# Masked cross attention: look-ahead, order of transfers and places of small work in a sequence

## The reference, cut to what matters

```python
def _L0_xattn_ref(target, source, target_mask, source_mask, Wq, bq, Wk, bk, Wv, bv):
    # b = 8, t = s = 512, SIZE = 256, HEADS = 16, HEAD_DIM = 16
    q = jnp.einsum('oc,bct->bot', Wq, target) + bq[None, :, None]
    k = jnp.einsum('oc,bcs->bos', Wk, source) + bk[None, :, None]
    v = jnp.einsum('oc,bcs->bos', Wv, source) + bv[None, :, None]
    ...
    dot = jnp.einsum('bhdt,bhds->bhts', q, k) / math.sqrt(HEAD_DIM)
    mask = target_mask[:, :, :, None] * source_mask[:, :, None, :]
    dot = mask * dot - (1.0 - mask) * NEG
    amap = jax.nn.softmax(dot, axis=-1) * mask
    out = jnp.einsum('bhts,bhds->bhdt', amap, v)
    return out.reshape(b, HEADS * HEAD_DIM, t)
...
x = _layernorm(x + _L0_xattn_ref(x, ctx_2048, mask, mask, Wq, bq, Wk, bk, Wv, bv), axis=-1)
```

## Time and profile before

| | |
|---|---|
| median of 3 runs | 3819.51 us (3816.24 to 3822.37) |
| the profiled execution | 3825.85 us, of which span 3824.0 us |
| masked cross attention in the span | about 454 us to 1323 us |
| busy in the whole span | PE 83%, PEld 54%, DVE 44%, ACT 33%, POOL 14% |
| mean granted clock of PE | 0.896 of full speed |

### The profile page before, as it was taken

The page is one execution under the profiler, slowest core; times in us unless marked ns, Lnnn a source line. Parts: engine busy times, 40 slices in busy tenths (PEclk is TensorE's granted clock), DMA queues, the critical chain, the costliest instruction groups (busy, mean ns, idle before and its releaser), DMA issues. The chain is left out here.

```text
span 3824.0 us, 48404 instructions
## 1 busy us (share of the span) xinstructions
PE 3156.5 (83%) x16306; PEld 2066.2 (54%) x16339; DVE 1683.5 (44%) x3232; ACT 1259.3 (33%) x3220; POOL 545.7 (14%) x551
## 2 busy tenths in 40 slices
PE   6999758777777659999987888599999997899894
PEld 5666422222222147777764555488888886444441
DVE  5666535444445321211115666366666665211113
ACT  2333214343435401111103444355565553211110
POOL 1000200111011120000000000233333332300002
PEclk9999867667767679999998999799999998999997
DMA  1000174444545140000001000211122102600323
GB/s 67 14 20 22 55 129 86 90 91 98 98 84 103 54 122 12 23 12 12 12 22 36 22 22 17 74 59 45 50 78 67 45 33 99 239 0 33 121 86 109
DMA packets 124210, 235.40 MB, mean 62 GB/s; under 512 B 10808, under 2 KB 23608, under 8 KB 124048
## 3 DMA queue, kind: packets, MB, share of 16 engines
q1 hardware_dynamic: 104928, 190.19, 18.6%
q0 software_dynamic: 7664, 27.40, 2.1%
q10 hardware_dynamic: 11456, 15.66, 1.3%
HBM read 161.55 MB, written 71.14 MB: 61 GB/s over the span
## 5 line engine op out<-in xcount | busy, mean ns | idle before, releaser
L1256 DVE TENSOR_REDUCE x_minus_max<-banks 128x2 f32<-128x1024 f32 x256 | 310.4, 1222 | 417.9 <-PE banks L1320 412.2
L1192 ACT ACTIVATE x_probs<-banks 128x512 f32<-128x512 f32 x512 | 287.7, 595 | 383.4 <-PE banks L1338 314.7
L1338 PE MATMUL banks<-x_stacked_q,x_stacked_k 53*128 53x512 f32 x512 | 267.9, 591 | 94.8 <-ACT x_probs L1192 68.5
L1338 PEld LDWEIGHTS banks<-x_stacked_q,x_stacked_k 53*128 53x128 f32 x512 | 106.0, 232 | 361.5 <-issue 190.5
L481 ACT ACTIVATE a_probs<-banks,a_minus_max 128x128 f32<-128x128 f32 (+1 forms) x512 | 209.0, 426 | 145.0 <-DVE a_minus_max L564 143.3
L1320 PE MATMUL banks<-x_stacked_k,x_stacked_q 51*128 51x512 f32 x512 | 217.7, 552 | 34.0 <-DMA x_stacked_q<-x_mask_parts_dram 28.6
L1350 PE MATMUL banks<-x_probs,x_v 128*32 128x512 f32 x1024 | 188.7, 819 | 5.4 <-ACT x_probs L1192 5.4
L2137 ACT ACTIVATE x_probs<-banks,x_minus_max,x_rroot 128x256 f32<-128x256 f32 x256 | 143.1, 567 | 91.4 <-DVE x_minus_max L2248 91.4
L2073 POOL TENSOR_TENSOR x_probs<-x_probs,x_inverse 128x512 f32<-128x512 f32 x128 | 133.1, 1040 | 275.6 <-DVE x_inverse L2282 275.6
L564 DVE TENSOR_REDUCE a_minus_max<-banks 128x2 f32<-128x512 f32 (+1 forms) x192 | 131.9, 687 | 82.3 <-remote 54.8
L2807 DVE TENSOR_TENSOR m_h<-banks,m_silu 128x512 f32<-128x512 f32 x39 | 27.0, 692 | 318.8 <-PE banks L2923 165.6
(11 more groups left out here) (369 smaller groups left out, 7737.6 us busy)
## 6 DMA issues: line engine op xcount, KB each, us to landing
x_parts_dram<-x_parts SPq DMA_DIRECT2D x16, 1024.0 KB, 5.4
x_x<-x_after SPq DMA_DIRECT2D x24, 512.0 KB, 4.4
x_stacked_k<-x_parts_dram SPq DMA_DIRECT2D x48, 256.0 KB
x_stacked_q<-x_parts_dram SPq DMA_DIRECT2D x48, 256.0 KB
x_after<-a_z SPq DMA_DIRECT2D x16, 512.0 KB, 2.7
x_z<-x_after SPq DMA_DIRECT2D x16, 512.0 KB, 6.6
x_heads_dram<-x_heads_out SPq DMA_DIRECT2D x32, 256.0 KB, 2.2
x_after<-x_z SPq DMA_DIRECT2D x16, 512.0 KB, 2.8
```

The source lines that it names most:

```text
L1192: act.activation(probs[:, n % 8, :], psum[at.bank(f"exp{n}")], ACT.Exp, scale=SCALE)\
L1256: dve.tensor_reduce(minus_max[:, c % 2, h % 4:h % 4 + 2, t], at.pair(use), AX.X, ALU.max, negate=True)\
L1338: ins = pe.matmul(psum[at.bank(use)], stacked[1][u][rows, h // 2, s * P:(s + 1) * P].bitcast(F32R), stacked[0][u][rows, h // 2, :].bitcast ...
```

## The change

Only this block is touched. Four things are changed. Scores run 36 slots ahead, so that score' begins at slot 28. Maxima and shifts move with them: the shift rows of a head group are now sent 17 slots before their first exp (slots 15, 31, 47, 63), and were sent 9 slots before (slots 7, 23, 39, 55). `stack` is split in two portions of four head pairs, with semaphores of their own; `load_inputs` stands between the portions and `load_rows` behind them. And the pieces of projection move from slots 24, 28, 40 and 44 to 34, 38, 42 and 51, the values pieces from 9 and 14 to 6 and 19.

```diff
-UNIT_LEAD = 28
+UNIT_LEAD = 36
 UNITS_IN_TAIL = 1
-MAXIMA_AT = 4
-SHIFT_AT = 7
+MAXIMA_AT = 12
+SHIFT_AT = 15
 SLOTS = 4 * 16
-PIECES_AT = (24, 28, 40, 44)
-VALUES_AT = (9, 14)
+PIECES_AT = (34, 38, 42, 51)
+VALUES_AT = (6, 19)
...
-            if q in (at, at + 16, at + 32):
-                add((kind, (q - at) // 16 + 1))
-            if q == at + 48:
-                add((kind + "'", 0))
+            if q in (at, at + 16):
+                add((kind, (q - at) // 16 + 2))
+            if q in (at + 32, at + 48):
+                add((kind + "'", (q - at) // 16 - 2))
...
-            def stack(b, u):
-                sp.wait_ge(parts_written, b * 32 + 32)
+            def stack(b, u, part):
                 for w in (1, 0):
                     for half in range(2):
                         for j, pair in enumerate(STACKED_PAIRS):
-                            sp.dma_start(stacked[w][u][HALF * half + CH * j:HALF * half + CH * (j + 1)],
-                                         parts_dram[w, u, pair[w]].rearrange("(h g d) s -> g d h s", g=2, d=CH)[half])\
-                                .then_inc(stacked_ready[w][u], 16)
+                            sp.dma_start(stacked[w][u][HALF * half + CH * j:HALF * half + CH * (j + 1), 4 * part:4 * part + 4],
+                                         parts_dram[w, u, pair[w], part * P:(part + 1) * P].rearrange("(h g d) s -> g d h s", g=2, d=CH)[half])\
+                                .then_inc(stacked_ready[w][u][part], 16)
...
                 if following:
-                    stack(b + 1, 1 - u)
+                    sp.wait_ge(parts_written, b * 32 + 64)
+                    stack(b + 1, 1 - u, 0)
+                if own and second:
+                    sp.wait_ge(v_ready, b * 2 + 2)
+                    load_inputs(b + 2, u)
+                if following:
+                    stack(b + 1, 1 - u, 1)
                 if own:
                     if not (isinstance(b, int) and b < 2):
                         sp.wait_ge(stored[u], at.in_turn * 16)
                     load_rows(b, u)
-                if own and second:
-                    sp.wait_ge(v_ready, b * 2 + 2)
-                    load_inputs(b + 2, u)
...
-                        if n == 0:
+                        if n in (0, 16):
                             for w in range(2):
-                                pe.wait_ge(stacked_ready[w][to], at.loads(ahead) * 8 * 16)
+                                pe.wait_ge(stacked_ready[w][to][n // 16], at.loads(ahead) * 8 * 16)
```

More of the change, by code:

```diff
@@ L961, in cross_attention_masked @@
         parts_written = sem("parts_written")
-        stacked_ready = [[sem(f"stacked_ready_{w}{u}") for u in range(2)] for w in "qk"]
+        stacked_ready = [[[sem(f"stacked_ready_{w}{u}{part}") for part in range(2)] for u in range(2)] for w in "qk"]
         v_ready = sem("v_ready")
@@ L1061, in stack @@
                         for j, pair in enumerate(STACKED_PAIRS):
-                            sp.dma_start(stacked[w][u][HALF * half + CH * j:HALF * half + CH * (j + 1)],
-                                         parts_dram[w, u, pair[w]].rearrange("(h g d) s -> g d h s", g=2, d=CH)[half])\
-                                .then_inc(stacked_ready[w][u], 16)
-                        sp.dma_start(stacked[w][u][HALF * half + STACKED_MASK:HALF * half + STACKED_MAX],
-                                     mask_dram[w, b].unsqueeze(1).broadcast_to([len(STACKED_PAIRS), H // 2, POS]))\
-                            .then_inc(stacked_ready[w][u], 16)
+                            sp.dma_start(stacked[w][u][HALF * half + CH * j:HALF * half + CH * (j + 1), 4 * part:4 * part + 4],
+                                         parts_dram[w, u, pair[w], part * P:(part + 1) * P].rearrange("(h g d) s -> g d h s", g=2, d=CH)[half])\
+                                .then_inc(stacked_ready[w][u][part], 16)
+                        sp.dma_start(stacked[w][u][HALF * half + STACKED_MASK:HALF * half + STACKED_MAX, 4 * part:4 * part + 4],
+                                     mask_dram[w, b].unsqueeze(1).broadcast_to([len(STACKED_PAIRS), H // 4, POS]))\
+                            .then_inc(stacked_ready[w][u][part], 16)
             def write_heads(b, u, c):
@@ L1261, in run @@
                         by_tile = minus_max[:, n % 2].rearrange("p (i g) t -> p t g i", g=2)
-                        at.wait_free(dve, f"score{8 * n + 7}" if kind == "maxima" else "score'7")
+                        at.wait_free(dve, f"score{8 * n + 7}" if kind == "maxima" else f"score'{8 * n + 7}")
                         high_part(dve, max_parts[:, :, :, 0, :], by_tile).then_inc(max_steps, 1)
```

## The result

The changed kernel takes 3694.7 us (median of 4 runs, 3690.0 to 3699.3), and the kernel before 3817.9 in the same comparison. The ratio is 0.968, with a 95% interval of 0.966 to 0.970. That is 123 us less, where I had forecast 98 (3721 us, range 3685 to 3765). The profiled execution took 3689.95 us with a span of 3688.1, 135.9 less than the span of the earlier trace rows. It is the quickest of the four runs, so its terms add up to more than the medians show.

What follows compares the result with a forecast made beforehand. No engine is full, so the order of waits bounds it, chiefly PE's for context and shift rows. Savings 87.5 + 6.2 + 4.5 = 98.2 us take the profiled 3825.85 to 3727.7, 6.3 over the median: 3721 us, range 3685 to 3765.

Steps and rivals of the forecast that it cites:

- Both waits: PE's waits for the context (69.1 us, nearly all in batches 1 to 5) and the shift rows (25.1 us) go.
- ACT's wait: At slot 24, for the inverse sums written at slot 20: PE's 5.8 us charged to each of batches 1 to 5, 29 us.
- A gain that hangs on the slot more than on the order: Projection pieces: from slot 34 even inputs landing no earlier (+45.9 us) would leave a wait of only 4 us.
- I put all this at nothing: Splitting `stack` in portions: 16 more transfers at 0.44 us issue each, 7 us, later second portion and z; cost nothing.
- the opening: Lead sequence before batch 0: first portion lands after 16.3 us, first exp at 542.3 instead of 546.8, 4.5 us gained.
- Rival C: Finer transfers are slow: portions land at +48 us, 116 us lost against 98 gained, 3837 us; chance 0.03.
- Pieces at nothing: New places of the projection pieces: work moved, not changed; still two pairs of neighbours four slots apart, so no effect.
- the middle batch: Batches 1 to 5: 89.7 us each, from batch 0's 87.0 less 3.1 plus 5.8, against 107.2; 87.5 us saved.
- 6.4 from the clock: Batches 1 to 5: the saving per batch beyond the waits, from a clock of 0.79 instead of 0.69.
- The rest: Outside batches 1 to 5: batches 0 and 6 lose shift waits, 6.2 us; first exp 4.5 us earlier; batch 7 unchanged.

Runs made afterwards that it cites:

- e4: The changed kernel with ACT's read of the inverse rows, and the wait ahead of it, at slot 29 instead of 24: 3674.2 us.
- e1: The changed kernel with the old order of transfers (both portions of stacked rows, z, then the inputs), its slots kept: 3698.1 us.
- e2: The kernel before with only the new order of transfers, in two portions; look-ahead 28, old shift and piece slots: 3705.2 us.
- e10: The kernel before with its stacked rows cut into two portions of half-size transfers, old order and slots kept: 3763.6 us.
- e5: The changed kernel with the projection pieces back at slots 24, 28, 40 and 44: 3775.5 us.
- e6: The kernel before with ACT's read of the inverse rows at slot 29 instead of 24: 3804.9 us.
- e11: The changed kernel with stacked rows in four portions of 64 KB transfers, inputs between the second and third: 3662.5 us.
- e13: The changed kernel with four portions, the inverse read at slot 29 and useless matmuls in batch 7: 3647.5 us.
- e7: The changed kernel with the old order of transfers (both portions first, inputs last) and the projection pieces at the old slots: 3833.4 us.

## Why the prediction was right, and where it was not

- **Both waits go.** Right: 69.1 and 25.1 us became 0.
- **ACT's wait takes their place.** Right in place and in count, and charged too high: 5.8 us a batch, and 4.0 to 4.5 was PE's wait, in batches 1 to 4 and 6. In batch 5 it was 1.25, where the clock had a mean of 0.66 from 970 to 989 us, just before it. So 29 us were charged to batches 1 to 5 and 18.0 were paid. e4 shows that this was all of it.
- **A gain that hangs on the slot more than on the order.** Right for the slot (e1, no wait), wrong in the comparison. The order at the old slots does nearly the same (e2, 11.5 us of the wait left). With the transfers cut in two, either of the two suffices, since each takes away the same wait: e1 and e2 lie 66 and 58 us under e10, and both changes together 69. With transfers of 256 KB neither was run, and at a landing of 45.9 us PE's slot 34 (+41.4 in e1) would still wait 4 or 5 us, by estimate.
- **The step that failed: "I put all this at nothing", on the portions' transfers.** Half-size transfers move the same bytes at 148 to 174 GB/s in batch 2, where it was 119 to 134. By e10 the cut is worth 60 us in the old slots, some 20 of them in the opening. The earlier first portion there I had counted, the quicker rate I had not. I took the issue cost as the only thing that 16 more transfers change. Rival C had the sign the wrong way round.
- **Pieces at nothing.** Wrong as a reading of the change. By itself the respacing gains little over the old slots (e2), but with shifts at 31 and 47 it is what keeps 81 us from being lost (e5). I compared the pieces with one another, and not with the other user of their bank.
- **The mis-sized term: the middle batch.** The forecast was 89.7 us, the measured length 84.7, which is 25 us over five batches, as much as the medians show over the forecast. By terms, 22.5 us a batch were saved and not 17.5. The two waits gave the 13.8 and 3.1 that I had taken, and ACT's wait cost 3.6 on average and not 5.8. The rest, which I had as 6.4 from the clock, was 9.2. PE's busy time for the same matmuls fell by 9.7 us a batch, from 400.6 us over the five to 351.9 (batches 2 to 5 of the kernel before are below, batch 1 is in the earlier trace rows). So the rest is the clock's in the main.

```profile
744.80:853.00 108.20, 81.55 (x310) 27.69 (x312) 48.27 (x57) 44.95 (x81) 13.34 (x11) 0.69 0.50 96
853.00:961.80 108.80, 77.97 (x309) 26.54 (x312) 47.39 (x57) 44.08 (x80) 13.34 (x11) 0.74 0.49 98
961.80:1066.80 105.00, 79.56 (x307) 26.85 (x306) 47.74 (x56) 44.36 (x81) 13.36 (x11) 0.71 0.48 95
1066.80:1173.90 107.10, 81.97 (x305) 27.34 (x304) 48.16 (x57) 44.79 (x81) 13.34 (x11) 0.68 0.47 96
```

  The forecast's base was batch 0 of one execution, 87.0 us at a clock of 0.79. In e6, where batch 0 runs the same instructions, it is

```profile
547.00:628.70 81.70, 68.96 (x306) 23.49 (x304) 44.71 (x48) 44.02 (x81) 8.91 (x7) 0.87 0.44 96
```

  From 81.7 the same sum (less 3.1, plus 5.8) gives 84.4, and with ACT's wait at its measured 3.6 it gives 82.2. So the base had drawn a low clock, and that 84.4 hits the measured 84.7 is in part luck. That the low clock of the base accounts for all of the term is worked out, not shown by a run of its own, and quicker transfers are in the measured length too.
- **The rest.** Batches 0 and 6 gave 8.2 and 5.6 us instead of 6.2 together, again in good part by the clock (0.85 and 0.88, before 0.79 and 0.83). From the start to batch 0's first context step it is 9.2 us (550.9 to 541.7) instead of 4.5, and batch 7 lost 1.4. In the opening the portion's landing was right (17.8 us after its first issue, forecast 16.3). But that issue came 2.6 us earlier than before (483.51 and 486.15), and from the first score to the first exp it took 35.7 us (501.26 to 536.91) and not 39.8. With 112.6 us of the middle batches that is 134.2 of the span's 135.9.

## What to carry to other kernels

Where several queues and slots cover one another's waits, price the wait that lies under the one you remove. It was there in a neighbouring batch, and in four of five batches it came back within 2 us of the price read off it. When a step of work moves, set its new slot against every other user of the bank it needs, not only against its own kind. And an unchanged number of bytes in more transfers is a change of its own: try the cut alone.

## What the runs showed of the hardware

- Stacked rows of 2 KB into 16 partitions moved at 119 to 134 GB/s in transfers of 256 KB (before, batch 2) and at 148 to 174 in transfers of 128 KB (batch 2 of the changed kernel, e1 and e10), all with the engines full (share over 1). In the lead sequence, with the engines full, the rates were 120 to 124 and 129 to 148. In transfers of 64 KB (e11) they moved at 121 to 155 GB/s with a share of 0.43 to 0.62. Only the number of such rows in a transfer differs.
- A 16 KB write on ACT's queue beside a full SP queue took 10.0 to 11.6 us until ACT could go on in the kernel before, and 9.3 to 10.2 in the changed one. With 64 KB transfers it landed within 5.7 us (e11) and 6.1 us (e13).
- Two useless matmuls in every second slot shortened a group of four exps from 4.61 to 3.15 us. The clock had been at its lower level (0.50) in the stretch where PE only followed ACT.
- Runs of one kernel spread by 8 to 37 us here (e7, ten runs from 3813.1 to 3849.9; the kernel before beside it, thirteen runs, 28 us), and the lengths of equal batches within one execution by 11 us (79.2 to 90.4), along with their clock.
